# Moving the value and gate projection between the near maxima, with its own tile for the transposed input

## The reference

```python
qkv = x @ Wqkv + bqkv                      # 16 heads of 16
scores = stack([einsum(q, shift(k, delta)) for delta in OFFSETS]) * scale + pos_bias
alpha = softmax(scores)                    # over the offsets
out = sum(alpha[i] * shift(v, delta_i))
gate = sigmoid(x @ Wgate + bgate)
x = layernorm(x + (flat(out) * gate) @ Wout + bout)
logits = relu(x @ rw1 + rb1) @ rw2 + rb2   # 8 experts
vals, ids = top_k(logits, 2); probs = softmax(vals)
pos = cumsum(one_hot(ids)) - 1             # tokens in order; at most 1024 are kept per expert
y = sum over k of probs[k] * expert[ids[k]](x)     # relu(x @ ew1 + eb1) @ ew2 + eb2
x = layernorm(x + y)
```

## Time and profile before

| | before |
|---|---|
| median of three runs | 1824.6 us |
| profiled execution | 1827.93 us, span 1826.2 us |
| PE busy | 1369.5 us, 75% |
| DVE busy | 965.3 us, 53% |
| ACT busy | 903.4 us, 49% |
| POOL busy | 696.3 us, 38% |
| granted clock of PE | 0.792 of 2.4 GHz |

### The profile page before, as it was taken

How to read it: one execution, slowest core, us unless ns; L and a number is a source line. 1 busy time by engine, 2 the same in 40 slices (tenths; PEclk the granted TensorE clock), 3 DMA queues, 4 the chain that set the end, 5 groups by cost and what they waited for, 6 DMA issues and landing times. The chain is left out here.

```text
span 1826.2 us, 69624 instructions
## 1 busy us (share of the span) xinstructions
PE 1369.5 (75%) x31232; PEld 872.2 (48%) x31232; DVE 965.3 (53%) x2122; ACT 903.4 (49%) x1552; POOL 696.3 (38%) x652
## 2 busy tenths in 40 slices
PE   0566697877878787787878778687653999999960
PEld 0234454544445454554545455454431566676640
DVE  3215365565547566565566556565462555555425
ACT  2243373544636454464655537364442766555526
POOL 2231243443526344363544436352342123222245
PEclk9766686877869787787877779686576999999985
DMA  9463352534335263443625334252203344444239
GB/s 214 95 179 91 103 115 83 148 90 119 91 96 139 76 151 76 108 95 86 138 80 133 72 103 103 85 125 65 60 16 87 111 96 94 107 110 96 36 35 368
DMA packets 195696, 195.14 MB, mean 107 GB/s; under 512 B 62847, under 2 KB 179663, under 8 KB 192160
## 3 DMA queue, kind: packets, MB, share of 16 engines
q1 hardware_dynamic: 177872, 167.18, 34.8%
q0 software_dynamic: 15360, 15.10, 5.3%
q10 hardware_dynamic: 2176, 8.52, 1.9%
HBM read 115.37 MB, written 86.25 MB: 110 GB/s over the span
## 5 line engine op out<-in xcount | busy, mean ns | idle before, releaser
L404 POOL TENSOR_TENSOR p<-p 128x512 f16<-128x512 f32 x96 | 131.0, 1365 | 285.9 <-ACT p L807 285.8
L827 ACT COPY featT<-gp 128x1024 f16<-128x1024 f16 x96 | 92.7, 1015 | 253.3 <-PE gp L552 253.2
L559 PE MATMUL gp<-featT,wr 128*128 128x512 f16 x768 | 196.1, 414 | 22.1 <-DVE mT L976 16.9
L1124 POOL DMA_INDIRECT disp<-y,sidx x128 | 176.4, 1378 | 52.3 <-issue 37.8
L404 DVE TENSOR_TENSOR p<-p 128x512 f16<-128x512 f32 x96 | 83.6, 871 | 204.9 <-ACT p L807 204.7
L1402 POOL DMA_INDIRECT xln<-y,place x64 | 103.5, 1617 | 220.6 <-DVE y L1544 202.1
L1440 PE MATMUL up<-rowsT,w 128*128 128x512 f16 x768 | 172.3, 385 | 9.2 <-DVE w L1517 5.4
L1454 PE MATMUL dn<-w,h 128*128 128x256 f16 x1536 | 170.1, 273 | 0.0
L806 ACT ACTIVATE p<-st 128x512 f16<-128x512 f32 x192 | 116.3, 606 | 87.6 <-PE st L584 43.3
L1454 PEld LDWEIGHTS dn<-w,h 128*128 128x128 f16 x1536 | 149.7, 98 | 17.3
L1501 ACT ACTIVATE h<-up,b 128x512 f16<-128x512 f32 x128 | 88.2, 689 | 130.1 <-PE up L1440 71.8
(11 more groups left out here) (174 smaller groups left out, 2700.8 us busy)
## 6 DMA issues: line engine op xcount, KB each, us to landing
v_near<-v_dram SPq DMA_DIRECT2D x32, 528.0 KB, 7.8
qk_dram<-qk SPq DMA_DIRECT2D x64, 256.0 KB, 3.4
o_dram<-o_far SPq DMA_DIRECT2D x64, 136.0 KB, 3.3
o_back<-o_dram SPq DMA_DIRECT2D x16, 544.0 KB, 3.9
v_dram<-vs SPq DMA_DIRECT2D x16, 528.0 KB, 3.3
v_far<-v_dram SPq DMA_DIRECT2D x64, 132.0 KB
disp<-y ACTq DMA_DIRECT2D x8, 1040.0 KB, 23.1
rows<-disp SPq DMA_DIRECT2D x16, 520.0 KB, 3.4
```

Source lines behind the costliest of these rows:

```text
L404: engine.tensor_tensor(p16[:, b, 1, :], p32[:, b, :], p16[:, b, 0, :], ALU.subtract).then_inc(is_split, 1)
L559: last = nc.tensor.matmul(dst, lhs(a, c), rhs(b, c), start=(k == 0), stop=(k == len(todo) - 1))
L827: gp_done(nc.scalar.copy(featT[:, i, :, :].rearrange("f c t -> f (c t)"), bank[:, :].bitcast(F16)), n, stage, PART_OF_T[stage], i)
L1124: nc.gpsimd.indirect_dma_start(out=disp[:, :], out_offset=bass.IndirectOffsetOnAxis(ap=sidx[:, t, k:k + 1], axis=0), in_=y16[n.par][:, t, ...
```

## The change

1. featT becomes two tiles, xT for the transposed input and rowT for og and y16. vg0 moves from slot 2 to slot 7, ahead of near1, and vg1 from slot 3 to slot 8, between near2 and near3. ACT takes vg0 one slot later instead of two. Scores of unit 3 move from slot 7 to slot 8.
2. Of the ranking, step c keeps the two instructions that read the bank; the others become a step d in slot 9, on DVE in slot 10.
3. For mT, DVE copies both halves out of the bank, releases it and takes the minimum in SBUF; SP waits for a semaphore of its own.
4. Of the eight clearings two stay in setup, three go to iteration -1 (slot 7), one each to slots 9, 11 and 13 of iteration 0.
5. In setup the q and k bias is loaded as rows on all partitions and picked with the identity on DVE, not regrouped through DRAM; the position bias is loaded first, on ACT's queue, and DVE builds its vectors before it splits the weights, with fewer copies; br2 is one load, not four; ks[1] is filled by POOL; nobody waits in setup for small biases and the stored vectors, the attention block does.

```diff
-CLEARED_IN_SETUP = 6
+CLEARED_IN_SETUP = 2
+CLEAR_AT = {(-1, 7): (2, 3, 4), (0, 9): (5,), (0, 11): (6,), (0, 13): (7,)}
...
-    0: [("proj", "qk0"), ("gate", "den1"), ("gate", "inv1")], 1: [("proj", "qk1"), ("gate", "mul")], 2: [("proj", "vg0")],
-    3: [("rank", "l"), ("proj", "vg1")], 4: [("outp", "t")], 5: [("rank", "c")],
+    0: [("proj", "qk0"), ("gate", "den1"), ("gate", "inv1")], 1: [("proj", "qk1"), ("gate", "mul")], 2: [],
+    3: [("rank", "l")], 4: [("outp", "t")], 5: [("rank", "c")],
     6: [("outp", "w"), ("maxp", "near0")],
-    7: [("outp", "y"), ("maxp", "near1")], 8: [("maxp", "near2"), ("maxp", "near3")],
-    9: [("maxp", "far0")], 10: [("maxp", "far1"), ("rout", "t"), ("split", "x")],
+    7: [("outp", "y"), ("proj", "vg0"), ("maxp", "near1")], 8: [("maxp", "near2"), ("proj", "vg1"), ("maxp", "near3")],
+    9: [("maxp", "far0"), ("rank", "d")], 10: [("maxp", "far1"), ("rout", "t"), ("split", "x")],
...
-LATER = {("act", "proj", "vg0"): 2, ("act", "proj", "vg1"): 2, ("act", "gate", "mul"): 2, ("act", "rank", "l"): 3,
+LATER = {("act", "proj", "vg1"): 2, ("act", "gate", "mul"): 2, ("act", "rank", "l"): 3,
...
-SCORES_AT = [-1, 0, 5, 7, 10, 12]
+SCORES_AT = [-1, 0, 5, 8, 10, 12]
...
-        featT = sb("featT", [P, 2, CT, N], F16)
+        xT = sb("xT", [P, 2, CT, N], F16)
+        rowT = sb("rowT", [P, 2, CT, N], F16)
...
-                    nc.vector.tensor_copy(m_nearT[:, :], view[:, 0:N]).then_inc(m_copied, 1)
+                    nc.vector.tensor_copy(m_farT[:, :], view[:, N:2 * N]).then_inc(m_copied, 1)
+                    gp_done(nc.vector.tensor_copy(mT[:, :], view[:, 0:N]), n, "maxp", "t", 0)
                     dve.wait_ge(m_copied, n.at(1, 1))
-
-                    gp_done(nc.vector.tensor_tensor(mT[:, :].rearrange("h (a r) -> h r a", r=FAR_STEP),
-                                                    view[:, N:2 * N].rearrange("h (r a) -> h r a", r=FAR_STEP),
-                                                    m_nearT[:, :].rearrange("h (a r) -> h r a", r=FAR_STEP), ALU.min), n, "maxp", "t", 0)
+                    drained(dve, n, "maxp", "t", 0)
+                    by_class = mT[:, :].rearrange("h (a r) -> h r a", r=FAR_STEP)
+                    nc.vector.tensor_tensor(by_class, by_class, m_farT[:, :].rearrange("h (r a) -> h r a", r=FAR_STEP), ALU.min).then_inc(m_ready, 1)
...
+                    gp_done(nc.vector.tensor_tensor(taken[:, :], bank[:, E * TILES:E * (TILES + 1)], taken[:, :], ALU.add), n, "rank", "c", 0)
+                elif part == "d":
+
                     dve.wait_ge(rexp_ready, n.at(1, 1))
                     nc.vector.tensor_scalar(rdiff[:, :], rexp[:, :], 1.0, None, ALU.add).then_inc(w_step, 1)
...
-                sp.dma_start(*loads[5], allow_slow_non_contiguous=True).then_inc(here[5], 16)
-                for u in range(4):
-                    src = g["bqkv"][D * (u // 2):D * (u // 2 + 1)].rearrange("(p e d) -> e d p", e=2, d=HD)[u % 2]
-                    sp.dma_start(g["bqk_dram"][u].rearrange("(d p) -> d p", p=PAIRS), src, allow_slow_non_contiguous=True).then_inc(regrouped, 16)
+                sp.dma_start(qk_bias, g["bqkv"][0:2 * D].partition_broadcast(P)).then_inc(qk_bias_in, 16)
                 for dst, src in loads[6:]:
-                    sp.dma_start(dst, src, allow_slow_non_contiguous=True).then_inc(loaded, 16)
-
-                sp.wait_ge(regrouped, 64)
-                sp.dma_start(a["bqk"][:, :], g["bqk_dram"].rearrange("u f -> f u"), allow_slow_non_contiguous=True).then_inc(loaded, 16)
+                    sp.dma_start(dst, src, allow_slow_non_contiguous=True).then_inc(a["biases_in"], 16)
...
-                sp.wait_ge(stored, 64)
...
+                for u in range(4):
+                    row = qk_bias[:, D * (u // 2):D * (u // 2 + 1)].rearrange("f (p e d) -> f e d p", e=2, d=HD)[:, u % 2]
+                    nc.vector.tensor_tensor(picked[:, u, :].rearrange("f (d p) -> f d p", p=PAIRS), row,
+                                            ident[:, :].rearrange("f (d p) -> f d p", p=PAIRS), ALU.mult).then_inc(bias_step, 1)
```

More of the change, by code:

```diff
@@ L386, in gp_done, with x_used, row_used @@
             instruction.then_inc(gp_drained[gp_slot(n, stage, part, k)[0]], 1)
[L388 to L397, removed]
+        def x_used(eng, n):
+            if n.c >= 1:
                 full(eng, n.shift(-1), "proj", "vg1", 1)
+        def row_used(eng, n):
+            if n.c >= 1:
+                full(eng, n.shift(-1), "rout", "h3", 1)
         def split_weights(eng, engine, n, k, e, is_split):
@@ L427, in head @@
                     sp.wait_ge(v_stored, n.at(16, 16))
+                    if n.i is None and n.c == 0:
+                        sp.wait_ge(pad_in, 32)
                     for u in range(2):
@@ L814, in tail, with transposed @@
                     evacuate_far(*pair_at(it, k, EVAC_AT))
-                if it.i is None and it.c == -1 and k == H - 1:
+                if it.i is None and (it.c, k) in CLEAR_AT:
                     act.wait_ge(rest_in[0], 64)
-                    for c in range(CLEARED_IN_SETUP, CLEARINGS):
+                    for c in CLEAR_AT[it.c, k]:
                         clear_slots(nc.scalar, disp, y16[0], c).then_inc(cleared, 16)
-            def transposed(n, stage, used):
+            def transposed(n, stage, dst, used):
                 for i in range(2):
@@ L826, in transposed @@
                         used()
-                    gp_done(nc.scalar.copy(featT[:, i, :, :].rearrange("f c t -> f (c t)"), bank[:, :].bitcast(F16)), n, stage, PART_OF_T[stage], i)
+                    gp_done(nc.scalar.copy(dst[:, i, :, :].rearrange("f c t -> f (c t)"), bank[:, :].bitcast(F16)), n, stage, PART_OF_T[stage], i)
             PART_OF_T = {"feat": "x", "outp": "t", "rout": "t"}
@@ L884, in rout @@
                 if part == "t":
-                    transposed(n, "rout", lambda: full(act, n, "outp", "w", 1))
+                    transposed(n, "rout", rowT, lambda: full(act, n, "outp", "w", 1))
                 else:
@@ L1183, in setup @@
                  (a["bo"][:, :], g["bout"].partition_broadcast(P)),
-                 (a["br1"][:, :], g["rb1"].rearrange("(u p) -> p u", p=P))] + \
-                [(a["br2"][:, t, :], g["rb2"].partition_broadcast(P)) for t in range(TILES)]
+                 (a["br1"][:, :], g["rb1"].rearrange("(u p) -> p u", p=P)),
+                 (a["br2"][:, :, :], bass.AP(g["rb2"].tensor, 0, [[0, P], [0, TILES], [1, E]]))]
         with nc.Block() as block:
@@ L1243, in _ @@
                 nc.gpsimd.memset(a["halfneg"][:, :], -0.5)
+                nc.gpsimd.memset(a["ks"][1][:, :, :].rearrange("p a t -> p (a t)").bitcast(FP32), TWO_ONES)
             @block.scalar
             def _(act):
+                nc.scalar.dma_start(*loads[5], allow_slow_non_contiguous=True).then_inc(here[5], 16)
                 for (src, h, _), k in zip(splits, (0,) * 9 + (1, 2, 3, 4)):
@@ L1271, in split @@
                     nc.vector.scalar_tensor_tensor(l, src, WS, h, ALU.mult, ALU.subtract).then_inc(lo, 1)
-                for k in range(11):
-                    split(k)
                 dve.wait_ge(here[5], 16)
```

72 lines of the change are left out of this document (43 added, 29 removed).

## The result

| | before | after |
|---|---|---|
| median | 1825.7 us (4 runs, 1817.1 to 1827.4) | 1869.8 us (4 runs, 1861.8 to 1873.2) |
| ratio to before, 95% interval | | 1.0245 (1.0199 to 1.0291) |
| profiled execution, span | 1826.2 us | 1868.1 us |
| PE busy | 1369.5 us | 1432.1 us |
| DVE busy | 965.3 us | 1010.1 us |

The change made the kernel slower by 44 us; 1821 was forecast, and 1869.8 lies above the range. Split by the starts of the q, k projections, the spans differ as follows. These starts are 56.27, 173.90 and 1200.40 us (batches 0, 2 and 15) before and 26.62, 163.92 and 1237.09 after.

A forecast was written before the change was run, and what follows sets the result against it. PE, busy 63.33 of 78.85 us in a steady iteration, and what it waits for were taken as the bound. Setup -22, first batches +10 and steady iterations +8 gave -4: 1824 profiled, 1821 as median, range 1793 to 1845.

The forecast's parts named there:

- its whole chain moves with the scores: Near maxima: o_back lands 11.1 us after the output projection's start as before, so at 835.7 instead of 838.74.
- vg1 2.75: Between near2 and near3: vg1's twelve products take 2.75 us at full clock; upper bound 2.5 us more at half clock.
- near1 waits for merge and vg0's evacuation: Near maxima: near1 reuses vg0's bank, so PE stands idle 3.5 us until the merge and one evacuation, to 837.5.
- what slots 2 and 3 give back: Between q, k and output projections: of 5.5 us of products removed, 3.0 us won, the output projection starting at 824.65.
- The limit set by ACT's far copy: Slots 2 and 3: the second far part overwrites banks o, which ACT's copy of the first frees at 817.75.
- the sum for the transposes: Second half of og's transposes: POOL's low half ready at 820.23, so they end near 820.85 instead of 822.98.
- the setup: Before the attention block: SP done by 28 instead of 50.73, mostly from fewer clearings, -22 us (-14 to -26).
- the early bank release: mT bank before the router: free 1.9 us sooner, PE's whole wait goes, 1.3 us an iteration.
- Rival C: Setup not shortened, because br1's 1024 small pieces block SP, not the clearings: -8 instead of -22, 1835 us; chance 0.08.
- the gaps shrink: PE's 1.77 us gap ending on "issue" amid scores: half taken as refilled by idle time, 0.9 us.
- First batches: Batches 0 and 1: the moved projection no longer runs under earlier waits, +6 and +4, sum +10 us (6 to 14).
- Rival B: Slower: vg1 runs at 1.2 GHz after the merge wait, +2.4 us an iteration, +24 in all, 1849 us; chance 0.21.

The follow-up runs named there:

- e5: After, with SP's stores and loads of the low parts of q and k issued behind the load of o_back: 1859.6 us, 1.0199 of before.
- e12: After, with DVE's merge one slot later and vg0 and vg1 one behind the other ahead of near1: 1823.8 us, 1.0007 of before.
- e3: After, with DVE's merge of the third unit one slot later, behind vg0's evacuation and the second near reduction: 1786.8 us, 0.9811 of before.
- e4: After, with vg0's 12 products computed twice into the same banks: 1863.4 us, 1.0238 of before.
- e2: After, with the scores of unit 3 back in slot 7, ahead of near1: 1828.1 us, 1.0065 of before.
- e8: After, with vg0 and vg1 back in slots 2 and 3, unit 3's scores in slot 7, and DVE's merge one slot later: 1761.7 us, 0.9675 of before.
- e1: After, with the move alone undone: vg0 and vg1 back in slots 2 and 3, unit 3's scores in slot 7: 1764.5 us, 0.9729 of before.
- e14: After, with vg0 and vg1 back in slots 2 and 3, DVE's merge one slot later, unit 3's scores kept in slot 8: 1769.7 us, 0.9655 of before.
- e13: After, without the move, with the ranking in one part and the late mT bank release: 1810.3 us, 0.9877 of before.
- e6: Before, with the move alone (two tiles, new slots for vg0 and vg1, unit 3's scores in slot 8): 1898.9 us, 1.0425 of before.

## Why the prediction was wrong, point by point

The chain that the prediction described is the one that decides, but two of its terms were too small. Means of the ten iterations, in us from the start of the q, k projection (the forecast counted from 805.60):

| start of | before | forecast | after |
|---|---|---|---|
| output projection | 21.2 | 19.0 | 19.2 |
| merge | 32.7 | 30.1 | 33.2 |
| near1 | 32.1 | 31.9 | 35.0 |
| far0 | 40.3 | 41.8 | 46.7 |
| next q, k projection | 79.0 | 79.4 | 82.5 |

far0 came 4.9 us later than forecast: 2.9 because the merge was later behind the output projection, 1.8 between near1 and far0, where vg1 stands. Behind far0, 1.8 us more came back than the forecast had; what gave them was not traced. This leaves the miss of 3.0 us an iteration.

- **Wrong step: "its whole chain moves with the scores".** The merge starts 14.0 us behind the output projection, not 11.1 (11.4 as a mean of before). o_back stands behind SP's transfers of q and k, which move with the q, k projection and not with the scores; e5 shows that. Put right alone (e5), it changes the time by only 8 us, within the uncertainty: near1 starts 2.1 us sooner then and still waits 3.8 us for the merge, and most of the gain is lost behind it.
- **Wrong step: "vg1 2.75" at full clock.** It took 5.30 us in the iteration shown and 4.8 as a mean of the ten, inside the bound of 2.75 + 2.5. The bound was right and the choice between the ends was not: all 384 products had run at full clock, but in a place where PE was dense. The row nearest to the new place was the stretch of maxima at 0.50. Here PE came from 8 us of idle and 5 us of small products. No run prices this term alone: e12 cured it and brought another wait.
- **Right in kind, not in size: near1 waits for merge and vg0's evacuation.** That was named, and e3, e4 and e2 show it. The prediction had 3.5 us an iteration for it; 5.0 were measured. It decides most of the time of the stage: one slot more for the merge is worth 79 us with the move and 10 us (0.5%, within the uncertainty) without it (e8 against e1), and it leaves 28 of the move's 94 us (e3 against e14). The prediction did not ask what that slot would bring.
- **Too high: what slots 2 and 3 give back.** 3.4 us in the iteration shown, 3.0 forecast; over ten iterations the mean is 2.0. The limit set by ACT's far copy was named, and PE waits 24.9 us for it over the program. In the sum for the transposes, 820.23 and half of 1.07 make 820.77 and not 820.85; this changes nothing.
- **A missing term, but hidden in after: the output projection's clock.** Its products take 319 to 351 ns as a mean in the runs with both halves in slots 2 and 3, and 373 to 401 in those with one half or both moved: +12.0 us over the program. The prediction counted PE's new idle time there as a chance to refill gaps only. In after these 12 us stand ahead of the wait for the merge, where 45.7 us of added work cost nothing in e4; they count once that wait is gone (e3).
- **Right: the setup and the early bank release.** Setup -29.7 (forecast -22, bound -26), 10.2 of it given back in the first batches; by e13 the net is 22 us, give or take 8. Rival C is out: the load issued behind br1's 1024 pieces took SP 0.67 us now, where it had taken 16.36. Which of the setup's edits did it was not tested one by one. The bank is worth 18 us, give or take 11; the forecast was 1.3 x 13 = 17.
- **Right: the gaps shrink.** The gaps on "issue" before near scores (L604 before, L606 after) fall from a mean of 1.90 us an iteration to 0.85; half of 1.77 was taken. By the rule cited from the Trainium skill, "Runtime: NRT & Kernel Launch", section "Instruction fetch mechanics", they would have stayed. What the gaps are, the runs do not show.
- **First batches.** Forecast +10, measured +19.7. The move's 9.5 was near the forecast; what failed is that the setup's gain was taken to arrive whole.
- **Rival B** was right in sign and mechanism, wait for merge and vg1 at 1.2 GHz. Its 1849 lacks the later o_back.

What stays open: how much of the wait comes from each of the merge's two causes (SP's order, and the chain behind the scores) when both are late together, since removing one (e5) only shows the other; and why o_back's transfers take longer beside those of q and k was not tried apart from the order.

## What to carry to other kernels

Before work is moved into a wait, ask what ends that wait and whether the moved work's own reader stands behind it on its engine: here one place in VectorE's order was worth 79 us, when the move had cost 94. Price a moved product at the clock of its new neighbours, and price the products that it leaves behind too, which lose the dense work ahead of them. A chain moves only as far as the slowest queue that it passes.

## What the runs showed of the hardware that was not expected

The granted clock stayed at 0.50 through 5.28 us in which PE was busy with 128x128x512 products the whole time (863.42 to 868.70), while twelve such products behind the output projection ran at 1.00.

Small operations of DVE became slow beside POOL's large ones. DVE's onehot (128x64) and chosen (128x32) in before, then in after, and POOL in after:

```profile
820.30 0.65 DVE L1038 TENSOR_TENSOR onehot<-expert_id,topf 128x64 f32<-128x64 f32 x1
820.98 0.56 DVE L1040 TENSOR_TENSOR chosen<-onehot 128x32 f16<-128x32 f32 x1
```

```profile
835.22 2.11 DVE L1042 TENSOR_TENSOR onehot<-expert_id,topf 128x64 f32<-128x64 f32 x1
837.36 2.24 DVE L1044 TENSOR_TENSOR chosen<-onehot 128x32 f16<-128x32 f32 x1
```

```profile
835.12 2.12 POOL L1141 TENSOR_TENSOR x<-og,x 128x1024 f16<-128x1024 f32 x1
837.21 2.34 POOL L1109 TENSOR_TENSOR xres<-xres,bo 128x1024 f32<-128x1024 f32 x1
```

Each DVE operation ends with the POOL operation that it ran beside, three to four times as long as before. The shortest onehot takes 0.22 us in both kernels; in before the one shown ran beside POOL's low parts of v (L1093). As a mean onehot takes 0.70 us before, 1.81 in after, 1.82 with the move alone (e6) and 0.67 with the move undone (e1): the move took the low parts of v out of POOL's queue there and brought these two side by side. What it costs was not measured by itself. The Trainium skill, "SBUF — State Buffer", section "SBUF: two separate sides", says that VectorE, with two inputs from SBUF, and GpSimd hold a pair of ports exclusively for a whole instruction; both DVE operations here read two, and the rows agree.
